# Unread products on TensorE in attention and in the gather, W2's squares ahead of the token table, the bias product on 128 rows

## The reference

```python
def _channel_attention(qm, km, vm, scale):        # 4 heads of 64 channels
    scores = jnp.einsum('bhdn,bhen->bhde', qh, kh) * scale
    attn = jax.nn.softmax(scores, axis=-1)
    out = jnp.einsum('bhde,bhen->bhdn', attn, vh)
    ...
att_global = _channel_attention(q * wqg + bqg, k * wkg + bkg, v * wvg + bvg, scale)
att_local = _channel_attention(q * wql + bql, k * wkl + bkl, v * wvl + bvl, scale)
return 2.0 * (att_global + att_local) * wp + bp
...
logits = xf @ gate_w                              # 2048 tokens, 8 experts
top_w, top_idx = jax.lax.top_k(logits, 2)
top_w = jax.nn.softmax(top_w, axis=-1)
h = jax.nn.gelu(jnp.einsum('td,edf->tef', xf, w1) + b1, approximate=False)
y = jnp.einsum('tef,efd->ted', h, w2) + b2
out = jnp.einsum('ted,te->td', y, combine)
...
x = x + _L0_xattn_ref(_layernorm(x), ctx_1024, ctx_1024, ...)
x = x + _L0_ffn_ref(_layernorm(x), ...)
```

## Time and profile before

| | us |
|---|---|
| median of three runs | 388.78 |
| the profiled execution | 388.25 |
| its span, first to last instruction | 386.3 |
| TensorE busy (products) | 357.4 |
| VectorE busy | 261.8 |
| ScalarE busy | 240.2 |
| GpSimd busy | 174.5 |

### The profile page before, as it was taken

One profiled execution on the slowest core, in us unless ns is written; L12 is line 12 of the kernel. 1 busy time (PEld: TensorE's weight loads), 2 busy tenths in 40 slices (PEclk: granted clock), 3 DMA queues, 4 the chain that ended last, 5 costly groups with the idle time before them and its releaser, 6 DMA issues.

```text
span 386.3 us, 11023 instructions
## 1 busy us (share of the span) xinstructions
PE 357.4 (93%) x3755; PEld 307.9 (80%) x3755; DVE 261.8 (68%) x600; ACT 240.2 (62%) x545; POOL 174.5 (45%) x189
## 2 busy tenths in 40 slices
PE   7599999999977987999999999999999999999980
PEld 2478787888867576998988988989889889898860
DVE  5986566466428879877777877778778765665630
ACT  4584556565623247888787886787778764655630
POOL 7874746473411121555353454453534534543331
PEclk9999999999999579999999999999999999999996
DMA  6976785698781011767786776877877877778521
GB/s 225 318 252 199 253 285 182 216 299 305 284 278 8 1 44 30 249 165 230 200 254 222 205 250 193 238 240 195 253 229 205 254 213 226 247 198 245 138 33 14
DMA packets 33807, 77.98 MB, mean 202 GB/s; under 512 B 10405, under 2 KB 23913, under 8 KB 27225
## 3 DMA queue, kind: packets, MB, share of 16 engines
q1 hardware_dynamic: 24088, 66.72, 49.1%
q0 software_dynamic: 7600, 10.48, 15.8%
q10 hardware_dynamic: 2066, 0.07, 0.3%
HBM read 30.55 MB, written 9.64 MB: 104 GB/s over the span
## 4 chain that ended last, share of the span: by engine, by line
PE 85%; DVE 6%; DMA 3%; issue 2%; ACT 1%; POOLq 0%; POOL 0%; DVEq 0%; ACTq 0%
PE bank L1064 26%; PE bank L1079 25%; PE bank L987 7%; PE bank L944 5%; PE bank L968 4%; PE bank L1040 4%; PE bank L1004 3%; PE bank L1011 2%; PE bank L976 2%; PE bank L1081 2%; PE bank L955 2%; PE bank L1028 2%; PE bank L985 1%; DMA shared<-xn_rows,row_of 1%; DMA out<-shared,row_of 1%
## 5 line engine op out<-in xcount | busy, mean ns | idle before, releaser
L482 POOL DMA_INDIRECT out<-shared,row_of x39 | 65.8, 1687 | 111.1 <-DMA out<-shared,row_of 62.4
L1079 PE MATMUL bank<-W,shared 128*128 (+1 forms) x936 | 108.6, 273 | 0.2 <-DVE shared L932 0.2
L1064 PE MATMUL bank<-shared,XR 128*128 128x128 f16 x1680 | 100.0, 218 | 0.4 <-issue 0.4
L1079 PEld LDWEIGHTS bank<-W,shared 128*128 128x128 f16 x936 | 89.7, 98 | 10.4 <-issue 0.4
L1064 PEld LDWEIGHTS bank<-shared,XR 128*128 128x128 f16 x1680 | 96.7, 97 | 1.5 <-issue 0.8
L601 ACT ACTIVATE shared<-shared 128x512 f32<-128x512 f32 x78 | 49.1, 629 | 51.1 <-DVE shared L915 50.3
L932 DVE SCALAR_TENSOR_TENSOR shared<-shared,XP 128x512 f16<-128x512 f32 x70 | 52.5, 750 | 26.4 <-ACT shared L603 26.4
L915 DVE SCALAR_TENSOR_TENSOR shared<-bank,XP 128x512 f32<-128x512 f32 x70 | 52.5, 750 | 24.4 <-PE bank L1064 18.7
L475 POOL DMA_INDIRECT shared<-xn_rows,row_of x39 | 40.5, 1038 | 40.5 <-DVE w_of L928 15.7
L603 ACT ACTIVATE shared<-shared,XP 128x512 f16<-128x512 f32 x70 | 50.6, 723 | 2.3
L865 DVE SCALAR_TENSOR_TENSOR W<-W,wscale (+1 forms) x32 | 40.8, 1280 | 4.3 <-ACT W L535 3.1
(11 more groups left out here) (166 smaller groups left out, 430.6 us busy)
## 6 DMA issues: line engine op xcount, KB each, us to landing
XR<-W SPq DMA_DIRECT2D x35, 1024.0 KB
W<-in_w SPq DMA_DIRECT2D x16, 1024.0 KB, 5.9
shared<-in_ctx_t SPq DMA_DIRECT2D x16, 256.0 KB, 3.1
W<-in_ctx SPq DMA_DIRECT2D x16, 128.0 KB, 5.2
out<-XR SPq DMA_DIRECT2D x16, 128.0 KB, 5.1
xn_rows<-W SPq DMA_DIRECT2D x16, 128.0 KB, 5.0
XR<-in_x SPq DMA_DIRECT2D x3, 512.0 KB, 5.7
shared<-xn_rows,row_of POOLq DMA_INDIRECT x39
```

Source lines behind the costliest of these rows:

```text
L482: pool.indirect_dma_start(out=out, out_offset=bass.IndirectOffsetOnAxis(ap=row_of[:, b:b + 1], axis=0), in_=Y[:, b % 2, :], in_offset=None ...
L1064: mm = pe.matmul(pHT[n][m][:, f % 4, :], first[:, c, w, f * P:(f + 1) * P], XT[:, n, v, c, :], start=(c == 0 and w == 0 and v == 0), stop= ...
L1079: pe.matmul(pY[n], hT[:, n, v, f, :], whole(Wh[:, slot, at:at + D]), start=(f == 0 and w == 0 and v == 0), stop=False)
```

## The change

It has six parts.

1. Unread products. `keep_busy(to, n)` multiplies a 128 x 128 matrix of ones by itself n times into a PSUM bank that holds nothing that is still needed. 28 of them stand behind the spread of q's factors, 12 in each of the steps 0, 1, 2, 6, 10, 13, 15, 16 and 17 of attention (the steps from 0 to 17 without squares, apart from the one with the scales' sum), 32 behind the table's products.
2. The bias products, `ones3` by B2 or B2s, run on 128 partitions. The 125 others hold zeros, which VectorE sets at the start.
3. k's factors come by two DMAs of 256 KB, already repeated for 128 partitions. TensorE spreads q's alone, and ScalarE's two copies are gone. q's first pass no longer waits for the inverse deviations, its second does.
4. All of W2's squares and their sum over partitions stand ahead of the table. ScalarE sums the fifth expert's before its first conversions, and makes the params, W2's half and the biases of the first expert ahead of the block loop. VectorE takes W2's scales right behind the table.
5. The token's number goes into a second pass over `ohB` (V, f16), and the 32 one-hots have one scalar instead of two.
6. Seven loads of W2 are issued one step later each (`FETCH`), the W1 scales one step earlier, each conversion in the blocks one block later, and the blocks' slots are worked out between the two halves of block 0.

```diff
-        FETCH = (0, 1, 2, 4, 5, 6, 8, 9, 10, 11, 12, 13, 14, 15, 16, 17)
+        FETCH = (0, 1, 2, 4, 5, 6, 8, 9, 10, 12, 13, 14, 15, 16, 17, 18)
...
@@ sync
             sp.wait_ge(bias_cut, 5)
+            sp.wait_ge(bias_zero, 3)
...
@@ gpsimd
                     if t == 0:
-                        pool.wait_ge(kc_ok, 1)
+                        factors(0, 1)
+                        pool.wait_ge(kw_in, 16)
...
@@ scalar
-            act.dma_start(rows, qk_rows).then_inc(rows_in, 16)
-            for n, to in enumerate((KW, KB)):
-                act.wait_ge(spread, n + 1)
-                act.activation(to.rearrange("p g d -> p (g d)"), ps[n][:, :], ACT.Copy).then_inc(kc_ok, 1)
+            act.dma_start(rows, q_rows).then_inc(rows_in, 16)
+            act.dma_start(KW.rearrange("p g d -> p (g d)"), ck[:, 0:2 * D]).then_inc(kw_in, 16)
+            act.dma_start(KB.rearrange("p g d -> p (g d)"), ck[:, 2 * D:4 * D]).then_inc(kb_in, 16)
...
-            for e in range(2, 4):
+            for e in range(2, 5):
                 square_sums(e)
...
-            for e in range(4, E):
+            for e in range(5, E):
                 square_sums(e)
+            act.wait_ge(scale2_ok, 3)
+            params(held["src"], spare_slot)
+            for n in range(2, 4):
+                high(n, held["src"], spare_slot, wscale[:, 1, held["src"]])
+            biases(held["src"], spare_slot)
...
-                if 0 <= i < CONVERTED - 4:
-                    u, g = i % 4, i // 4
+                if 1 <= i < CONVERTED - 3:
+                    u, g = (i - 1) % 4, (i - 1) // 4
...
@@ vector
-            dve.memset(ones3[:, :], 1.0).then_inc(filled, 1)
+            dve.memset(ones3[:, :], 0.0).then_inc(bias_zero, 1)
...
+            dve.wait_ge(bias_zero, 1)
+            dve.memset(ones3[0:3, :], 1.0).then_inc(filled, 1)
+            dve.memset(B2[:, :, :], 0.0).then_inc(bias_zero, 1)
+            dve.memset(B2s[:, :, :], 0.0).then_inc(bias_zero, 1)
...
-                    dve.wait_ge(rs1_ok, rs1_calls(tq))
-                    dve.wait_ge(spread, 4)
+                    dve.wait_ge(spread, 1)
...
-            dve.tensor_tensor(ohB, iotaBX, blk_h[:, :].rearrange("p (o t) -> p o t", o=1).broadcast_to([P, NB, N2]),
-                              ALU.is_equal).then_inc(ohb_ok, 1)
+            chain(dve.tensor_tensor(ohB, iotaBX, blk_h[:, :].rearrange("p (o t) -> p o t", o=1)
+                                    .broadcast_to([P, NB, N2]), ALU.is_equal))
+            dve.tensor_tensor(V, ohB, tokens.rearrange("p (o t) -> p o t", o=1).broadcast_to([P, NB, N2]),
+                              ALU.mult).then_inc(v_ok, 1)
             for t in range(N2):
-                dve.tensor_scalar(ohR[:, t, :], iotaR[:, :], slot_f[:, t:t + 1], tokens[:, t:t + 1],
-                                  ALU.is_equal, ALU.mult).then_inc(ohr_ok, 1)
+                dve.tensor_scalar(ohR[:, t, :], iotaR[:, :], slot_f[:, t:t + 1], None, ALU.is_equal).then_inc(ohr_ok, 1)
...
@@ tensor
+            def keep_busy(to, n):
+
+                for _ in range(n):
+                    pe.matmul(to, ones[:, :], ones[:, :], start=True, stop=True)
...
+            pe.wait_ge(filled, 8)
+            keep_busy(pGram[:, 3, :], 28)
...
                     squares(pGram[:, w % 4, :], w).then_inc(gram_ok, 1)
+                elif 0 <= i < T + 2 and i != SUMS1:
+
+                    done = sum(1 for p in PRODUCT if p < i)
+                    after(pe, trace_ok, done // 4)
+                    if i > SUMS1:
+                        pe.wait_ge(scale_step, 1)
+                    keep_busy(pGram[:, 3, :], 12)
...
-            for e in range(2, 5):
-                squares_of_second(e)
...
-            for e in range(5, E):
+            for e in range(2, E):
                 squares_of_second(e)
             pe.wait_ge(trace2_ok, E)
             pe.matmul(pSum[:, 2 * E:], ones32[:, :], wsq[:, 2 * E:], start=True, stop=True).then_inc(wsum2_mm, 1)
+
+            pe.wait_ge(v_ok, 1)
+            for t in range(2 * T):
+                pe.wait_ge(ohr_ok, t + 1)
+                pe.matmul(pTok, ohR[:, t, :], V[:, :, t], start=(t == 0), stop=(t == 2 * T - 1)).then_inc(table_mm, 1)
+            keep_busy(pGram2[0], 32)
```

89 lines of the change are left out of this document (44 added, 45 removed).

## The result

| | us | runs |
|---|---|---|
| before | 388.70 | 385.82 to 389.31 |
| changed | 361.44 | 358.27, 359.13, 363.76, 370.10 |
| forecast | 369.0 | range 362 to 392.5 |

The changed kernel is faster: 0.9242 of the time before, 95% interval 0.9161 to 0.9322. All ten have a median of (364.40 + 368.53) / 2 = 366.5 us, so 361.44 is a favourable draw: by the ten the gain is 22.2 us and the time lies inside the range.

What follows compares the result with a forecast made beforehand. The prediction took TensorE, at the low clock level throughout attention, as the bound. From the profiled 388.25 us, start -0.9, attention at the high level -15 and routing -3.2 gave 369.1 us; range 362 to 392.5.

Steps and rivals of the forecast that it cites:

- Reading the level: TensorE in attention: its first 123 us ran at the lower clock level (1.2 GHz), despite the printed 1.00.
- A: Attention: the clock level rises by the first tiles and stays; 369 us, range 362 to 378, chance 0.46.
- against it: Attention's start: burst too short, a gap of 1.5 to 2 us follows, and fp32 products never lifted the level.
- C: Attention: level rises at the start and falls in a thin step, or rises late; 379 us, chance 0.14.
- Attention at the high level: Attention's steps: saving at the high clock level, bounded by other engines and DMA; -15 us, bounds 0 and -21.
- near 5.3 us: Attention: a squares' step of this length, with DMA share over 0.9, would show the level had risen and stayed.
- costs what it did on three: Bias products: running them on 128 rows takes the same time as on three; no term in the sum.
- Start: Up to the first scores: near 11.0 us instead of 11.91, so -0.9; bounds -1.8 and +1.6.
- Routing: Table, first gather and first blocks: -0.7 - 1.0 - 1.5 = -3.2 us, bounds -0.5 and -5.5.
- A block costs 5.9 us before and after: Expert blocks behind block 3: TensorE's time per block stays at 5.9 us, so no saving there.
- B: Attention: level stays low to its end and the twelve products cost TensorE time; 391.7 us, chance 0.34.
- D: Attention: level is high, but weights, x and ctx come late through DMA; 386 us, chance 0.06.

Runs made afterwards that it cites:

- a_again: The changed kernel, unaltered, run six more times; median 368.63 us (358.12 to 374.55).
- a_bias3: The changed kernel with the bias products back on three rows, all unread products kept; median 361.32 us.
- a_halfcopy2: The changed kernel with the copy of a block's W1 half cut to half its bytes from block 6 on; median 356.64 us.
- a_slotonce: The changed kernel with TensorE loading a slot's register only once, for block 4, and using it for all later blocks; median 361.01 us.
- a_moredma: The changed kernel with one more 256 KB DRAM-to-DRAM transfer, awaited by nobody, in each of attention's 16 steps; median 363.58 us.
- a_none: The changed kernel without any unread product and with both bias products back on three rows; median 388.13 us.
- a_nofill: The changed kernel without any unread product (no 28, 12s or 32), bias products still on 128 rows; median 379.63 us.
- b_fill_bias128: The kernel before plus attention's unread products and the bias products on 128 rows; start, loads and routing as before; median 363.96 us.
- a_early: The changed kernel with the weights' conversions in the blocks from block 0 on, as before the change, instead of block 1; median 366.22 us.
- b_fill: The kernel before plus attention's unread products alone (28 and nine times 12), bias on three rows; median 389.31 us, 375.2 over ten executions.

## Why the forecast was wrong

**Reading the level.** Right: the print of 1.00 in attention was not what it ran at, and A came true in kind: squares at 57 ns, no records before, records inside now. It rose at 21.5 us though, not behind the 28, whose 3.17 us lay hidden in the hole as said. In four other profiles (a_again, a_bias3, a_halfcopy2, a_slotonce) it did rise right behind them, at 9.1 to 9.7 us, and fell 3.4 us later, behind the gap that A's "against it" names. And it fell again at 76.1, as C had it. A and C are not two cases: the ten executions lie anywhere from 358 to 375.

**The step that failed: "Attention at the high level".** -15 us was the sum of "eight steps save 1.5 each and four 0.7", bounded at -21 by "0.78 x 103.1 = 80.4 us of full DMA". The profiled execution gave -25.7 with a third of attention at the low level. The eight steps with squares gave 55.0 - 31.7 = 23.3 us, 2.9 each; the thin steps 6, 10 and 13 gave 0.2, 0.2 and 0.9 (4.98, 4.98 and 4.26 us instead of 5.17), the rest 1.0. The term rested on the DMA share: 5.4 us of full DMA in a squares' step made "near 5.3 us" its floor. The step shown took 3.72 us, at a share of 1.05; a_moredma lost nothing. By rate over share the queues moved 251 / 0.78 = 322 GB/s in the step of rows 2, 379 / 1.05 = 361 in this one and 399 / 1.03 = 387 in a_moredma: the share says that they are in use, not how much they still could do. What the rows did offer as a bound was each other engine's own work: in attention VectorE, the busiest, has 62.96 us of it, which allows a saving of 40, and 3.6 to 4.7 us a step, where the steps with squares came to 4.0 in the mean.

**Luck in the number.** A also had the level stay high to the end, and in no profile did it: a_again's profile has 35 of 86.9 us of attention at the high level and saves 16.3, near the -15. So the median of the ten, 366.5 us, is close to 369 because two errors work against each other: a step at the high level saves about twice what was said, and the level is high for less of attention than A assumed.

**The bias product "costs what it did on three".** Wrong in the change's favour: 0.4 us less a step in attention, 0.25 us less a block. The pauses around a product of three rows were in the trace (0.62 us where 0.48 are needed), and I read only the product's own duration. In attention it is 5.5 us at the low level (a_none to a_nofill), less at the high one; in the blocks it would have been 0.25 x 35 = 8.8 us. Between a_none and a_nofill 4.5 us of that are there behind block 3's transposes, against the kernel before nearly nothing, for the reason below.

**Start.** -0.9 forecast, +0.6 measured. Timeline of the start (start us, us, engine, line, what):

```profile
2.59 1.02 DVE L647 MEMSET B<- 128x1152 uint32 x1 [0.19 <-issue]
...
3.80 1.02 DVE L648 MEMSET B2s<- 128x1152 uint32 x1 [0.19 <-issue]
...
6.36 3.17 PE L963 MATMUL bank<-ones 128*128 128x128 bf16 x28
...
9.89 0.71 DVE L728 SCALAR_TENSOR_TENSOR shared<-XR,mv,bank 128x512 f32<-128x512 f32 x1
...
11.37 0.43 DVE L621 BATCH_NORM_STATS2 st<-XR 128x6 f32<-128x256 f32 x1 [0.76 <-DMA XR<-in_x]
...
11.71 0.73 DVE L740 SCALAR_TENSOR_TENSOR shared<-shared,rs,bank 128x512 f32<-128x512 f32 x1
```

The memsets are the 2.0 us worked out and TensorE is free at 6.4 us, as said. VectorE's list is what is late behind them: the statistics of the next tiles stand ahead of q's first pass (9.89; 10.09 before), and those of one more tile, which waited 0.76 us for x, ahead of its second (11.71), which the first scores wait for. Whether x comes late for the 0.5 MB more of factors, which the prediction had in its bound of +1.6, wasn't tried. In a_none first scores came at 11.47, in the other variants of the changed kernel at 11.3 to 12.4.

**Routing.** -5.4 against -3.2, at the edge of its bounds (-5.5): 1.1 to the table's end (0.7 said), 1.6 from there to block 0's products (1.0), 2.7 to block 3's transposes (1.5, bound 2.4). Timeline of TensorE:

```profile
94.56 5.68 PE L957 MATMUL bank<-W 128*128 128x128 bf16 x96
102.57 0.39 PE L1052 MATMUL bank<-wsq,ones 128*128 128x8 f32 x2 [2.33 <-ACT bank L534]
102.81 4.03 PE L1057 MATMUL bank<-XR 128*128 128x39 f16 x32
106.66 3.60 PE L963 MATMUL bank<-ones 128*128 128x128 bf16 x32
110.64 0.45 PE L1066 MATMUL bank<-ident,shared 128*128 128x128 f32 x2 [0.39 <-DMA shared<-xn_rows,row_of]
...
112.82 4.47 PE L1090 MATMUL bank<-shared,W 128*128 128x128 f16 x48
...
122.78 0.38 PE L1066 MATMUL bank<-ident,shared 128*128 128x128 f32 x2
```

Squares at 59 ns, ScalarE's sums the wait behind them as named, the table from 102.81 to 106.84. Last logits to this end is 16.8 us; 133.0 less 115.07 were 17.9. The level rose at 110.2, as the 32 products ended, and fell at 113.6: block 0's products took 4.47 us, hidden as forecast and useless here. From them to block 3's transposes 9.96 us, below the 10.3 counted. The one-hots, in VectorE's groups:

```profile
L866 DVE TENSOR_SCALAR XR<-iotaR,slot_f 128x128 f16<-128x128 f16 x32 | 5.3, 246 | 0.0
L863 DVE TENSOR_TENSOR XR<-XR,tokid 128x1248 f16<-128x1248 f16 x1 | 0.8, 808 | 0.0
```

246 ns each, 5.3 / 32 = 0.165 us apart (0.17 said), the second pass 0.81 us: both prices hold. The Trainium skill, "VectorE: DVE Perf Modes", tier table, agrees with this row: the prediction's estimate of 190 ns from its figures and 60 ns for the one scalar left make 250.

**Blocks.** "A block costs 5.9 us before and after": right as a number, for a wrong reason, as the floor fell and pauses filled it. It also undid the routing. b_fill_bias128 has neither the moved squares nor the other parts from 3 on, and reached 357.51: to block 3's transposes it is 6.8 us slower than the changed kernel (39.61 against 32.77 from the last logits), behind them 7.5 us faster (226.2 against 233.7). Its waits ahead of the products with W1 are 0.6 us there. a_none says the same: 4.7 us won up to block 3's transposes (33.52 against 38.18), 5.4 lost behind them (238.48 against 233.05). So parts 3 to 6 are worth nothing net as they stand, as far as single profiles tell. Which of them brings the load's pauses, that b_fill_bias128 hardly has with the load at the same place, stays open; it isn't the later conversions, since a_early still waits 3.8 us there.

**Rivals.** B (391.7): neither profile of the changed kernel had the level low throughout attention; the nearest is a bad execution of b_fill (392 to 398), whose profile had 14 us at the high level. D is refuted by a_moredma.

## What to carry to other kernels

Before pricing a clock change, price every engine's own work in a step at both levels, and take the slowest of them as the floor; a DMA share near 1 wasn't one here. Read pauses around an instruction as part of its price: here a product on three rows and a register load between two runs of products cost beside their own duration. Before putting a rise of the clock down to a change, count how often the kernel before shows it. When one execution decides nothing, take what it is made of (here us at the high level) and fit over all profiles.

## What was not expected of the hardware

- The same kernel's attention had 35 us at the high level in one profiled execution and 55 in the other, and its times spread 358.12 to 374.55 us (4.5%). The Trainium skill, "TensorE: Matmul & The Clock Gate", Part 1, says that the switch varies between runs of the same kernel and puts what the ramp costs at under 1% of a typical span; the variation is seen here, the 1% isn't.
- TensorE, 97.3 of 103.1 us busy, stayed at the low level throughout in the profiled execution, with fp32 products and squares. With 28 and nine times 12 bf16 products of 128 rows and columns added (b_fill) no execution of ten has the mean clock of such a one.
- In every profile in which it had risen it was low again for part of 76 to 113 us, where attention ends and the routing begins, with the unread products and without.
- A register load on TensorE beside a 1 MB copy cost up to 0.9 us in the changed kernel; behind the 2.7 us of products, at most 0.3. In the kernel before the same pair cost at most 0.2.
